# Two of sixteen tiles' roots of degree fetched by GpSimd in a graph network's weighted sums

## What is computed

```python
def _gcn(x, W, b, row, col, ew):
    xw = x @ W
    deg = jax.ops.segment_sum(ew, col, num_segments=N) + 1.0
    dinv = jax.lax.rsqrt(deg)
    norm = dinv[row] * ew * dinv[col]
    agg = jax.ops.segment_sum(norm[:, None] * xw[row], col, num_segments=N)
    agg = agg + (dinv * dinv)[:, None] * xw
    return agg + b
```

## Time and profile before

| | |
|---|---|
| runs | 8155.06, 8195.37, 8196.05 us; median 8195.37 |
| profiled execution | 8190.61 us, span 8188.5 us |
| PE busy | 4791.9 us (59%) |
| VectorE (DVE) busy | 3941.0 us (48%) |
| GpSimd (POOL) busy | 3647.7 us (45%) |
| ScalarE (ACT) busy | 2873.3 us (35%) |
| granted TensorE clock, mean | 0.692 |
| first edge stage, about | 150 to 2676 us |
| first weighted sum, about | 2726 to 3336 us |
| second edge stage, about | 3450 to 6310 us |
| second weighted sum, about | 6410 to 7050 us |
| count stage and the end, about | 7050 to 8188 us |

### The profile page before, as it was taken

One profiled execution on the slowest core, in us unless ns is written; L12 is line 12 of the kernel. 1 busy time (PEld: TensorE's weight loads), 2 busy tenths in 40 slices (PEclk: granted clock), 3 DMA queues, 4 the chain that ended last, 5 costly groups with the idle time before them and its releaser, 6 DMA issues. The chain is left out here.

```text
span 8188.5 us, 172048 instructions
## 1 busy us (share of the span) xinstructions
PE 4791.9 (59%) x41016; PEld 3521.6 (43%) x41016; DVE 3941.0 (48%) x17687; ACT 2873.3 (35%) x5415; POOL 3647.7 (45%) x5091
## 2 busy tenths in 40 slices
PE   2111111111111588578878888877888588599997
PEld 1000000000000476455555555555555476478886
DVE  3233333333233788533333333333333688788886
ACT  2222222222222455322223222222223355566664
POOL 3566666666665011255555555555554011412222
PEclk6555555555555667777778777778777666699998
DMA  4555555555555477455555555555554577300000
GB/s 124 133 140 141 140 141 143 137 138 138 140 141 134 145 223 221 139 163 160 160 158 168 160 160 163 161 159 161 160 158 135 144 221 219 99 1 0 0 0 32
DMA packets 1010949, 1117.36 MB, mean 136 GB/s; under 512 B 216892, under 2 KB 749475, under 8 KB 1010440
## 3 DMA queue, kind: packets, MB, share of 16 engines
q1 hardware_dynamic: 652056, 516.07, 21.3%
q0 software_dynamic: 155136, 423.83, 19.5%
q10 hardware_dynamic: 203680, 176.57, 7.7%
HBM read 877.11 MB, written 238.87 MB: 136 GB/s over the span
## 5 line engine op out<-in xcount | busy, mean ns | idle before, releaser
L810 POOL DMA_INDIRECT counts<-tab_pr,idx x1616 | 1547.8, 958 | 1300.3 <-PE pu L1030 726.8
L810 POOL DMA_INDIRECT counts<-tab_p,idx x1616 | 1555.1, 962 | 933.4 <-issue 556.1
L1070 PE MATMUL pz<-tmpb,pieces 96*128 96x64 bf16 x1616 | 138.7, 236 | 1951.0 <-issue 1154.3
L884 DVE BATCH_NORM_STATS2 st<-pz 128x6 f32<-128x64 f32 x1616 | 252.5, 219 | 1543.5 <-remote 882.2
L1070 PEld LDWEIGHTS pz<-tmpb,pieces 96*128 96x128 bf16 x1616 | 94.5, 121 | 2022.7 <-issue 2022.7
L1030 PE MATMUL pu<-pieces,tmpb 96*128 96x512 f32 x808 | 625.0, 866 | 435.1 <-ACT pieces L1156 349.3
L1040 PE MATMUL pz<-wz,pieces 96*128 96x65 f32 x3232 | 718.5, 308 | 87.7 <-ACT pieces L1159 84.4
L890 DVE TENSOR_TENSOR pieces<-counts,pz 128x256 f32<-128x256 f32 x404 | 169.5, 420 | 1243.2 <-remote 992.7
L1414 POOL TENSOR_TENSOR acc<-acc,pieces 128x32 f32 x808 | 198.4, 246 | 1133.7 <-issue 1028.9
L1041 PE MATMUL pz<-wv,pieces 128*128 128x65 f32 x3232 | 699.1, 302 | 0.0
L1471 PE MATMUL pz<-counts,pieces 128*128 128x286 bf16 x4557 | 682.5, 284 | 0.1
(11 more groups left out here) (318 smaller groups left out, 10115.9 us busy)
## 6 DMA issues: line engine op xcount, KB each, us to landing
kept_d<-counts SPq DMA_DIRECT2D x808, 256.0 KB
counts<-kept_d SPq DMA_DIRECT2D x808, 256.0 KB
pieces<-rel_d ACTq DMA_DIRECT2D x808, 192.0 KB
counts<-srcp_d SPq DMA_DIRECT2D x808, 64.0 KB
counts<-tab_p,idx POOLq DMA_INDIRECT x1616
counts<-tab_pr,idx POOLq DMA_INDIRECT x1616
tmpb<-tab_q ACTq DMA_DIRECT2D x808, 12.0 KB
tmpb<-tab_s ACTq DMA_DIRECT2D x404, 16.0 KB
```

What stands on the lines that cost most here:

```text
L810: pool.indirect_dma_start(out=rows[:, par, u, j, 0:width], out_offset=None, in_=table, in_offset=bass.IndirectOffsetOnAxis(ap=idx[:, 2 * h ...
L884: nc.vector.bn_stats(st16[:, u * SUB + j, :], z[:, j, 0:ED])
```

## The change

POOL now fetches `dinv` of the sources for the last FETCHED = 2 of a step's 16 tiles by indirect DMA from a DRAM copy, `dinv_d`, straight into `wd`. PE does not look these two tiles up, DVE does not pick them. `wd` becomes double. The fetch for step it+2 stands in POOL's program ahead of the wait and adds of step it; those for steps 0 and 1 stand ahead of all steps. `weigh` waits for the fetched columns too. `degrees` has SP store `dinv` once DVE has it.

```diff
+    FETCHED = 2
...
+        dinv_d = dram("dinv_d", (NPAD, 1))
...
-        wd = sb("wd", [P, U * SUB])
+        wd = sb("wd", [P, 2, U * SUB])
...
+        s_dinv = [sem(f"dinv_fetched{k}") for k in range(2)]
...
+            def tiles_of(u):
+
+                return SUB - FETCHED if u == U - 1 else SUB
...
                                 for k in range(3):
                                     for h in range(2):
+                                        if j >= tiles_of(2 * q + h):
+                                            continue
                                         mm = nc.tensor.matmul(looked[2 * q + h][:, j * HT:(j + 1) * HT],
...
-                                        if j == SUB - 1 and k == 2:
+                                        if j == tiles_of(2 * q + h) - 1 and k == 2:
                                             mm.then_inc(s_look, 1)
...
-                    def pick(it, u):
+                    def pick(it, par, u):
...
-                        for j in range(SUB):
+                        for j in range(tiles_of(u)):
...
-                    def weigh(it):
+                    def weigh(it, par, k):
                         dve.wait_ge(s_pick, done(it * U + U - 1))
-                        nc.vector.tensor_tensor(wr[:, :], wd[:, :], ew[:, ds(it * NS, NS)], ALU.mult).then_inc(s_w, 1)
+                        dve.wait_ge(s_dinv[par], 16 * FETCHED * (k + 1))
+                        nc.vector.tensor_tensor(wr[:, :], wd[:, par, :], ew[:, ds(it * NS, NS)], ALU.mult).then_inc(s_w, 1)
...
+                        pool.wait_ge(s_pads, 1)
                     pool.sem_inc(s_acc, CREDIT + U)
 
+                    def fetch_dinv(it, par, k):
+                        if k is not None:
+                            pool.wait_ge(s_dinv[par], 16 * FETCHED * k)
+                            pool.nop(nofuse=True)
+                        nc.gpsimd.tensor_copy(idx[:, par, 0:FETCHED], idx_all[:, ds(it * NS + NS - FETCHED, FETCHED)]
+                                              ).then_inc(s_idx, 1)
+                        pool.wait_ge(s_idx, it + 1)
+                        pool.nop(nofuse=True)
+                        if k is not None:
+                            pool.wait_ge(s_w, done(it - 2))
+                            pool.nop(nofuse=True)
+                        for f in range(FETCHED):
+                            pool.indirect_dma_start(
+                                out=wd[:, par, NS - FETCHED + f:NS - FETCHED + f + 1], out_offset=None, in_=dinv_d,
+                                in_offset=bass.IndirectOffsetOnAxis(ap=idx[:, par, f:f + 1], axis=0)
+                            ).then_inc(s_dinv[par], 16)
+                    fetch_dinv(0, 0, None)
+                    fetch_dinv(1, 1, None)
+
                     def step(it, par, k, before, left):
+                        if left > 2:
+                            fetch_dinv(it + 2, par, k + 1)
                         pool.wait_ge(s_staged, done(it))
...
+            dinv_at = 1 if again else 3
...
                     sp.wait_ge(s_load, loads)
+                    sp.wait_ge(s_dve, dinv_at)
+                    sp.dma_start(dinv_d.rearrange("(p t) o -> p (t o)", t=NT), dinv[:, :]).then_inc(s_keep[0][0], 16)
+                    sp.wait_ge(s_keep[0][0], 16)
```

More of the change, by code:

```diff
@@ L321, in build @@
                     s_split, s_code, s_upper, s_stats2, s_var2, s_sqrt2, s_scaled2, s_norm2,
-                    s_part, *s_parted]
+                    *s_dinv, s_part, *s_parted]
         assert sorted(s.num for s in all_sems) == list(range(all_sems[0].num, all_sems[0].num + len(all_sems)))
@@ L1377, in pick @@
                                 looked[u][:, j * HT:(j + 1) * HT], ALU.is_equal, ALU.mult,
-                                accum_out=wd[:, u * SUB + j:u * SUB + j + 1])
+                                accum_out=wd[:, par, u * SUB + j:u * SUB + j + 1])
                         last.then_inc(s_pick, 1)
-                    def weigh(it):
+                    def weigh(it, par, k):
                         dve.wait_ge(s_pick, done(it * U + U - 1))
-                        nc.vector.tensor_tensor(wr[:, :], wd[:, :], ew[:, ds(it * NS, NS)], ALU.mult).then_inc(s_w, 1)
+                        dve.wait_ge(s_dinv[par], 16 * FETCHED * (k + 1))
+                        nc.vector.tensor_tensor(wr[:, :], wd[:, par, :], ew[:, ds(it * NS, NS)], ALU.mult).then_inc(s_w, 1)
                     def hot_of(it, par):
@@ L1395, in step @@
                         for u in range(U):
-                            pick(it, u)
-                        weigh(it)
+                            pick(it, par, u)
+                        weigh(it, par, k)
                         hot_of(it, par)
```

## The result

| | before | after |
|---|---|---|
| median, runs side by side | 8175.22 us | 8589.04 us |
| lowest to highest, 4 runs each | 8150.51 to 8196.05 us | 8584.91 to 8592.23 us |
| span of the profiled execution | 8188.5 us | 8589.2 us |

The ratio is 1.0499 with an interval of 1.0477 to 1.0522: slower by about 414 us. The direction was forecast, the size was not: 8589 lies above the predicted 8389 and above the range's upper end of 8550.

What follows compares the result with a forecast made beforehand. The prediction took a 5.65 us load loop across engines, near DVE's 5.57 floor, as the bound. A three-step loop of 15.16 + 5.75 = 20.91 us added 1.01 a step, +198 on 8190.6: 8389 us, range 8290 to 8550.

Steps and rivals of the forecast that it cites:

- load loop: Products, SP's kept rows, source codes, ACT's one-hots, fold staging, next-but-one products: 11.30 us for two steps, 5.65 a step, without DVE.
- Picks and look-ups at nothing: Two picks fewer save DVE at most 0.50 us a step, outside the bounding loop; PE's 6 fewer look-up products count nothing.
- The store of the roots, the other stages at nothing: SP's store of dinv costs nothing beside a 6.69 us multiplication; edge and count stages stay within noise.
- The fetch stands behind the adds of step a, so it isn't ahead at all: In POOL's order, step a's adds leave 0.57 us before w(a+3), the weights' multiplication, for the whole fetch.
- that closes a loop of three steps: From w(a), the weights' multiplication, through loads, one-hots, fold, adds and fetch to w(a+3): 20.91 us, 6.97 a step; chance 0.83.
- the 2.48 from the first kept load to the codes: Within the three-step loop, SP's kept rows to its source codes take 2.48 us, left as found.
- upper bound of 23.68: High case of the three-step loop: 16.44 as found plus a 7.24 us fetch, 7.89 a step, 8569 us.
- The fetch, 5.75: On POOL, last add to the second issue's end 3.54 us, then a landing of 2.2 us: 5.75 in all.
- Unchanged pieces: Loop parts outside the fetch: products 1.27 us after the weights' multiplication instead of 2.55, other parts left as found.
- POOL nearly the second bound, 6.73: POOL's own sequence per step: 1.68 us to the first add, 1.51 adds, 3.54 fetch, close to the 6.97 pace.
- Stretched issue: Rival: each indirect DMA takes its longest beside DVE work, POOL's step becomes 7.77 us, +355 us, 8545; chance 0.07.
- The range: 8290 to 8550 us: the loop's lower bound with unseen slack, most of the way to its upper, half of stretched issue.

Runs made afterwards that it cites:

- no_fetch: The changed kernel without any fetch, the two tiles' columns set to one once: 7018.90 us beside 7019.56 for the kernel before on that chip, ratio 1.0002.
- fetch_unused: The changed kernel with all 16 look-ups and picks kept, its fetches sent to a tile nobody reads: 7051.68 us, on a chip where before takes 7019.56.
- after_all_lookups: The changed kernel, but PE looks all 16 tiles up again while DVE still picks 14: 8614.17 us.

## Why the prediction missed

- **What bounds the kernel before**: right in its path. The load loop was given 5.65 of 5.96; opening it alone brought 5.59. But most of that loop is SP's own issuing, and this stays at 5.59 a step when the loop is open, beside DVE's floor of 5.57.
- **Picks and look-ups at nothing**: right. `no_fetch` puts the ceiling at a ratio of 1.0002.
- **The store of the roots, the other stages at nothing**: right, 399.1 of 400.7 us lie in the two sums.
- **The fetch stands behind the adds of step a, so it isn't ahead at all**: right, and the direction with it. Moving it four ahead took the pace from 7.99 to 6.29.
- **The failed step is "that closes a loop of three steps"**, with 15.16 us to the last add. It took the fold's path through the kept rows, codes and one-hots, and took slack out of it. But PE's order puts the fold of step a behind the products of a+1. As soon as w is late by the fetch, those products are late, the fold with them, and the loop closes over two steps. In the step that the prediction read, the last add ended 16.44 after w (mean of the sum 17.06); the prediction shortened that to 15.16, while it grew to 17.72 (mean). By the sum: 17.72 + 6.24 = 23.96 for three steps, where 20.91 stood. That is 3.05 too little, of which 2.56 is this path and 0.49 the fetch.
- **The predicted path was itself too short**, by 1.47 of these 2.56. In the 40 of 90 steps where ACT staged the fold straight behind the one-hots, so that it did hold, the last add ended 16.63 after w. The term at fault is the 2.48 from the first kept load to the codes: 4.36 there, since each of the four kept loads now waits for its own products; codes to ACT took 3.44 in place of 4.05. As an estimate, 16.63 + 6.24 is 7.62 a step for a loop of three alone; the rest up to 7.99 is the second loop's. That 23.96 falls close to the prediction's own upper bound of 23.68 (16.44 as found, landing 3.7) is luck: there the path was long because slack wasn't removed.
- **The fetch, 5.75**: 6.24 measured. Last add to first issue 1.33 (1.35 forecast), both issues 2.28 (2.19), issue end to w 2.63 (2.2 for the landing). The landing varied from 1.38 to 3.97, a little past both bounds of 1.64 and 3.7.
- **Unchanged pieces**: w to products 1.31 (1.27 forecast); PE's products and fold 1.92 and 1.79 on average at a clock of 0.54, where they took 1.71 and 1.38 at 0.71. The prediction had no term for a slower PE.
- **POOL nearly the second bound, 6.73**: wrong. `fetch_unused` does the same work in the same order at 6.01, so the times that were added up overlap: there the first add follows the staged fold by 1.71 too, but the second issue still runs for 0.90 of it.
- **Stretched issue**: did not happen in the changed kernel; 975 ns on average, and 19 of 404 took over 1.1 us. It isn't nothing where the step is denser: 1036 on average in `fetch_unused`, 85 of 404 over 1.1 and the longest 1.50, with DVE at work 447 of 520 us. The Trainium skill, "SBUF — State Buffer" (the trap "DVE blocks DMA"), says that DVE's two-port modes hold up the issue of such a DMA; no run here shows whether these longer issues come from that. The Trainium skill, "DMA: Bandwidth & Descriptors" (section "Anatomy of one DMA — SWDGE (gpsimd) path"), gives about 2.0 us of fixed cost for a DMA issued by GpSimd. From the start of the second issue to w it took 0.95 + 2.63 = 3.6 here, beside loads that held the DMA engines at 0.55.
- **The range**: its upper end was taken between bounds of one and the same loop. A second loop was not among the rivals.

## What to carry to other kernels

A prefetch is as far ahead as its issuing engine's place in the pipeline, not as its step index says: an in-order engine that waits for step a's end before it fetches for a+2 delivers nothing early. When a change makes an instruction late, list what stands *behind* its consumers on each in-order engine, even without a data dependence, and look for the shortest loop that closes through them; then divide by its number of steps. Time that looks like slack before the change may be removed only if nothing on that path hangs on the instruction that will be late. Before pricing a relief, find the loop that bounds the step: here an order of loads (0.8% gained) mattered, and two picks of sixteen did not. And count the issuing queue among the engines: its issues are in no busy row, yet eight of them filled a step of 5.59 us.

## What was unexpected of the hardware

- Indirect DMAs of 128 words, issued well ahead and read by no one, slowed the step from 5.93 to 6.42 us (two of them a step), though they move almost nothing: SP's four loads of codes took 3.59 us to issue in place of 3.10. On another chip they stayed at 3.10.
- An indirect DMA that moves 4 bytes a partition kept POOL for 975 ns on average, one that moves whole rows 958 to 962; its price is the issue, not the bytes.
- Two things went with a lower granted clock. One is PE's waiting: 0.71 before, 0.54 after, and `after_all_lookups` left it at 0.56. The other is six look-up products fewer in a step: on one chip `no_fetch` had 0.61 and `fetch_unused`, with all of them and nearly the same pace, 0.68.
- Two chips differ by 14% on the same program (8175 against 7020 us). The first sum starts some 390 us earlier on the faster one, and its pace is nearly the same: 5.91 in `no_fetch` there, 5.96 in the kernel before here.
